# Two small VectorE operations written as operations of two tensors: the norms' clamp and the cast of a pair's tokens

## The chip, the cores and the metric

The kernel runs on one core of a Trainium2 chip. The metric is the device time of one execution in microseconds, the median of the runs shown. A core has TensorE (PE in the profile; its weight loads are PEld), VectorE (DVE), ScalarE (ACT), GpSimd (POOL) and SyncE (SP), which here only issues DMAs. Each engine works through its own list of instructions in order; semaphores tie the lists together.

## The reference

4096 tokens (16 sequences of 256) of width 128 pass through four stages, each preceded by a layer norm and added to its input: linear attention, a feed-forward part, column attention, and the same feed-forward part again. The feed-forward part is the one that matters here. It has two layers, and each layer is a local attention and an MLP:

```python
h = shift_token(x)
q, k, v = jnp.split(h @ wqkv, 3, axis=-1)          # 8 heads of 64
q = q / jnp.clip(jnp.linalg.norm(q, axis=-1, keepdims=True), 1e-12) * qs
...                                                # k likewise, with ksc
q, k = rotary_xpos(q, k)
o = local_attention(q, k, v)                       # windows of 64, softmax
x = x + o @ wo
...                                                # then shift, norm, w1, gelu gate, w2
```

The clamp of a norm is the `clip`: the kernel takes the larger of the sum of squares and 1e-24.

## The kernel before, in words

The program is a row of blocks: front and linear attention, then for each feed-forward part two attention blocks (`attention_block`) and two MLP blocks (`mlp_block`), and the column attention between the two parts. So there are four attention blocks and four MLP blocks. In every block each engine has a list of its own, written out by hand, and `wait_ge` and `then_inc` set the waits. There is no planner: the order in the code is the order on the engine.

Tokens are handled in 8 pairs of sequences (512 tokens each) and 32 tiles of 128 tokens. The attention loop runs over `i`; in its turn `i` an engine works on scores, softmax and output of unit `i` (or `i - 1`) and on the projections, rotary products and norms of tile `j = i + 5`. The parts that the change and the prediction's steps touch:

- **The cast** (`high_parts`, L458, DVE). A pair's shifted tokens `hs` (128x512, float32, in `K.rn[:, 1]`, put there by a DMA) are cast to float32r as `hhi`. POOL then takes the remainder `hlo` (`low_parts`, L516), and PE multiplies both parts with the weights (L384 to L386). It runs once a pair. In each attention block six casts are in the loop, at the end of DVE's turn for `i` = 0, 4, ... 20. The first two pairs' casts come earlier: for the first layer of a part in the entry of its attention block, between the layer norm's products (L714), and for the second layer within the MLP block before it (`early`), after x = 6 and x = 12.
- **The clamp** (`norms`, L439, DVE). L435 sums the squares of a tile's q and k per head into `ss16` (128x16, SBUF), L439 clamps them into `ssc`. It runs once a tile, 128 times in all. ACT takes the logarithm (L786) and the exponential (L790) of it, giving the factors `rnt`, and goes on with the squares of the next tile (L468). In the MLP blocks POOL raises `ssc` to the power -0.5 instead (L915); that is ten of the 128.
- **DVE's turn** in the loop: L426 (sine product of q), L700 twice (maxima), L706 (copy of transposed probabilities), L416 twice and L426 (the other rotary products), L435, L439 (the clamp), L710 (inverse sums), L449 (copy of keys), once a pair L719 (residual), and once a pair L458 (the cast).
- **POOL's turn**: L842 twice (probabilities times inverse sums, 128x512 each, released by L710), L507 twice (rotary sums times the norms' factors), once a pair L516, L498 twice (rotary sums of the tile ahead). All of these read and write SBUF.
- **ACT's turn**: L468 twice (squares), L478 (copy of values), L776 (copy of the other half of the transposed probabilities), eight exponentials (L768), L782, L488, L786, L790.
- **PE** transposes the probabilities (L621) as soon as each half of L842 is done, and among others does L406 (transposes), L611 (scores), L640 and L658.

Other lines that are spoken of: L277, a subtraction of two SBUF tensors into float32r on DVE in the norm before the column attention; L1081, L1083 and L1093 on DVE, L319, L327 and L329 (tables and weight parts for the next attention) on POOL in the MLP and entry stages; L568, the centring product of PE in the entry, which waits for L714 to free its bank.

Of the kernel before, what the change touches and what calls it, by code (L numbers as in the profile page):

```python
# [18 lines left out]
ALU = mybir.AluOpType  # L19
AX = mybir.AxisListType  # L20

P = 128
# [5 lines left out]
HEADS, DH, WINDOW = 8, 64, 64  # L28
# [8 lines left out]
NORM_MIN = 1e-24  # L37
# [41 lines left out]
def front_block(nc, K, A):  # L79

    S = K.s
# [6 lines left out]
    with nc.Block() as block:  # L88
        @block.sync
        def _(sp):  # L90
            x = d["L0_attn_a_x"].rearrange("b (u p) c -> p (b u) c", p=P)
            sp.dma_start(K.ident[:], d["c_ident"]).then_inc(S.ident_in, 16)
            for j in range(2):
                sp.dma_start(K.tok[:, 4 * j:4 * j + 4, :], x[:, 4 * j:4 * j + 4, :]).then_inc(S.x_in[j], 16)
            sp.dma_start(K.cent_w[:], d["c_cent"]).then_inc(S.cent_in, 16)
            sp.dma_start(K.mean_w[:], d["c_mean"]).then_inc(S.mean_in, 16)
            for j in range(2, PAIRS):
                sp.dma_start(K.tok[:, 4 * j:4 * j + 4, :], x[:, 4 * j:4 * j + 4, :]).then_inc(S.x_in[j], 16)
            sp.dma_start(masks[:, 0:2 * P], d["c_mask"]).then_inc(S.mask_in, 16)
            for r in range(2):  # L100
                sp.dma_start(masks[64 * r:64 * r + 64, 2 * P:4 * P], d["c_mask"][64 - 64 * r:128 - 64 * r]).then_inc(S.mask_in, 16)
            load_linear_weights(sp, K, A)

        @block.gpsimd
        def _(pool):
            pool.memset(K.eps[:], EPS_LN).then_inc(S.eps_set, 1)
            pool.memset(K.ssb[:], SS_BIAS)
            pool.memset(K.mhalf[:], -0.5)
            pool.memset(K.rsb[:], float(20.0 * np.log(2.0)))
            clear_linear_tiles(pool, K, A)  # L110
            for p in range(PAIRS):
                pool.wait_ge(S.ln_hi, p + 1)
                pool.tensor_tensor(K.LO[:, pair(p)], K.lnf[:, p % 2], K.HI[:, pair(p)].bitcast(F32), ALU.subtract).then_inc(S.ln_lo, 1)
# [317 lines left out]
def norms(dve, K, n, j):  # L431

    S = K.s
    dve.wait_ge(S.f_sq, 2 * TILES * n + 2 * j + 2)
    dve.tensor_reduce(K.ss16[:], K.sq.rearrange("p w (h d) -> p (w h) d", d=DH), AX.X, ALU.add).then_inc(S.f_ss, 1)  # L435
    dve.wait_ge(S.f_ss, TILES * n + j + 1)
    if j >= 1:
        dve.wait_ge(S.f_rn, TILES * n + j)
    dve.tensor_scalar(K.ssc[:], K.ss16[:], NORM_MIN, None, ALU.max).then_inc(S.f_cl, 1)  # L439


def keep_keys(dve, K, n, j, bank):
# [9 lines left out]
def high_parts(dve, K, n, q):  # L452

    S = K.s
    dve.wait_ge((S.f_h0, S.f_h1)[q % 2], 16 * PAIRS * n + 32 * (q // 2 + 1))
    if q >= 2:
        dve.wait_ge(S.f_v, TILES * n + 4 * (q - 1))
    dve.tensor_copy(K.hhi[:, q % 2], K.hs[:, q % 2]).then_inc(S.f_hi, 1)  # L458


def squares(act, K, n, j, banks):
# [409 lines left out]
def mlp_block(nc, K, n):  # L871
# [11 lines left out]
    with nc.Block() as block:  # L883
# [186 lines left out]
        def _(dve):  # L1070
# [32 lines left out]
            def early(x):  # L1103
                s, r = divmod(x - 8, 3)
                if x == 8:
                    dve.wait_ge(S.wa_tab, n + 2)
                if x in (6, 12):
                    high_parts(dve, K, n + 1, (x - 6) // 6)
                if 0 <= s < LEAD:
                    if r == 0:  # L1110
                        times_sin(dve, K, n + 1, s, 0, K.pt)
                        times_cos(dve, K, n + 1, s, 0, K.pt).then_inc(S.f_m, 1)
                    if r == 1:
                        times_cos(dve, K, n + 1, s, 1, K.pt)
                        times_sin(dve, K, n + 1, s, 1, K.pt).then_inc(S.f_m, 1)
                    if r == 2:
                        norms(dve, K, n + 1, s)
                if (x - 7) % 3 == 1 and 2 <= (x - 7) // 3 < LEAD + 1:
                    keep_keys(dve, K, n + 1, (x - 7) // 3 - 2, K.ss)
# [25 lines left out]
def clear_linear_tiles(pool, K, A):  # L1145

    pool.memset(A.bd[:], 0.0).then_inc(K.s.a_zero, 1)
    pool.memset(A.k2[:], 0.0)
    pool.memset(A.v[:], 1.0)
    pool.memset(A.eps[:], A_EPS)  # L1150
# [760 lines left out]
def linear_attention(nc, K):  # L1911
    with split_parts(nc, K, "linear"), ExitStack() as ctx:
        def sb(name, shape, dt=F32):
            return ctx.enter_context(nc.sbuf_tensor("linear_" + name, shape, dt))

        A = Bag()
        A.w = sb("w", [P, 4, P])
        A.b = sb("b", [P, 3])
        A.eps = sb("eps", [P, 1])
        A.bv = sb("bv", [P, P])  # L1920
        A.hm = sb("hm", [P, 16])
        A.bd = sb("bd", [P, 4 * A_F])
        A.w_hi = sb("w_hi", [P, 3, P], F32R)
        A.w_lo = sb("w_lo", [P, 3, P], F32R)
        A.q = sb("q", [P, 2, PAIR])
        A.k = sb("k", [P, 2, PAIR])
        A.v = sb("v", [P, 2, 4, A_M, 32])
        A.kp = sb("kp", [P, 4, A_HEADS * A_F])
        A.qp = sb("qp", [P, 2, A_M, PAIR])
        A.kvs = sb("kvs", [P, PAIR])  # L1930
        A.k2 = sb("k2", [P, 2, 2, A_M, 32])
        A.lnd = sb("lnd", [P, PAIR])
        A.rd = sb("rd", [P, PAIR])
        A.on = sb("on", [P, PAIR])
        front_block(nc, K, A)
        linear_attention_block(nc, K, A)


def column_attention(nc, K):
    with split_parts(nc, K, "column"), ExitStack() as ctx:  # L1940
        def sb(name, shape, dt=F32):
            return ctx.enter_context(nc.sbuf_tensor("column_" + name, shape, dt))

        B = Bag()
        B.w = sb("w", [P, 4, P])
        B.b = sb("b", [P, 4])
        B.bs = sb("bs", [P, 2])
        B.w_hi = sb("w_hi", [P, 3, P], F32R)
        B.w_lo = sb("w_lo", [P, 3, P], F32R)
        B.full = sb("full", [P, 2, PAIR])  # L1950
        B.hi = sb("hi", [P, 2, PAIR], F32R)
        B.lo = sb("lo", [P, 2, PAIR], F32R)
        B.qs = sb("qs", [P, 2, B_G, B_RUN], F32R)
        B.ks = sb("ks", [P, 2, B_G, B_RUN], F32R)
        B.kh = sb("kh", [P, 2, B_RUN // B_T, SEQ], F32R)
        B.E = sb("E", [P, 8, 2, SEQ])
        B.nm = sb("nm", [P, 8, 2])
        B.dn = sb("dn", [P, 8, 2])
        B.rd = sb("rd", [P, 4, 4, 2, 4])
        B.r = sb("r", [P, SEQ])  # L1960
        B.z = sb("z", [P, 2, SEQ])
        B.sel = sb("sel", [P, 2, P])
        B.dm = sb("dm", [P, B_T])
        B.o = sb("o", [P, SEQ])
        B.scr = nc.dram_tensor("qk_parts", [SEQS, B_ROWS, 4, B_DH, B_G, B_RUN], F32, kind="Internal").ap()
        norm_block(nc, K, 2, split=True, column=B)
        column_attention_block(nc, K, B)


def build(nc, d, out):  # L1970
    with ExitStack() as ctx:
        K = Bag()
        K.d, K.out = d, out
        K.s = Semaphores(lambda name: ctx.enter_context(nc.semaphore(name)))

        def sb(name, shape, dt=F32):
            return ctx.enter_context(nc.sbuf_tensor(name, shape, dt))

        def ps(name):
            return ctx.enter_context(nc.psum_tensor(name, [P, 512], F32))  # L1980

        K.X = sb("X", [P, TOK])
        K.Y = sb("Y", [P, TOK])
        K.tok = K.Y[:].rearrange("p (j c) -> p j c", c=P)
        K.ident = sb("ident", [P, P])
        K.identb = sb("identb", [P, P], BF16)
        K.mask = sb("mask", [P, 2, 2 * P], BF16)
        K.mean_w = sb("mean_w", [P, P])
        K.cent_w = sb("cent_w", [P, P])
        K.eps = sb("eps", [P, 1])  # L1990
        K.ssb = sb("ssb", [P, 1])
        K.mhalf = sb("mhalf", [P, 1])
        K.rsb = sb("rsb", [P, 1])
        K.colp = sb("colp", [P, 3])
        K.rn = sb("rn", [P, 2, 2, PAIR])
        K.pa = sb("pa", [P, 2, 2, PAIR])
        K.pb = sb("pb", [P, 2, 2, PAIR])
        K.rsum = sb("rsum", [P, 2, 2, PAIR])
        K.lnq, K.lnl, K.lnr, K.lnf = K.pb[:, 0], K.pb[:, 1], K.rsum[:, 0], K.rsum[:, 1]
        K.proj = [ps("proj0"), ps("proj1")]  # L2000
        K.sc = [ps("sc0"), ps("sc1")]
        K.pt = [ps("pt0"), ps("pt1")]
        K.ss, K.ob = ps("ss"), ps("ob")

        linear_attention(nc, K)
        ffn(nc, K, 0)
        column_attention(nc, K)
        ffn(nc, K, 1)
# [15 lines left out]
```

## Time and profile before

| | us |
|---|---|
| median of 3 runs | 1874.98 (1874.9 to 1876.33) |
| the profiled execution, whole | 1867.61 |
| its span, first to last instruction | 1865.8 |
| busy: PE / DVE / ACT / POOL | 1701.5 / 1376.7 / 1315.6 / 1117.5 |

The profile is of one execution. Its rows give start and duration of instructions, the idle time of the engine before each, and what ended that idle time. Consecutive instructions of an engine overlap by some tens of nanoseconds in the records, and PE's ends are modelled. The time of a POOL instruction is recorded more roughly than the others'. A duration counts from the start that is recorded to the end, so if an instruction is held up within the engine, its duration grows and no idle time is shown.

### The profile page before, as it was taken

What the parts mean: (1) busy time and instruction counts of PE and PEld (TensorE: products, weight loads), DVE (VectorE), ACT (ScalarE), POOL (GpSimd) and SP (SyncE); (2) the same over time, 40 slices, a digit from 0 to 9 for tenths busy, and PEclk for the clock granted to TensorE, in tenths of its full rate; (3) what the DMA queues carried; (4) which work ended last, traced back from release to release, by engine and by line L of the source; (5) the groups of instructions that cost most, each with busy time, mean ns of one, the idle gap of its engine ahead of it and who ended that gap; (6) DMA issues with size and microseconds to landing.
All of it is one profiled execution on the core that took longest, in us unless ns stands there. A gap on an engine that the chain in (4) does not pass through costs nothing. (4 is left out here: it accounts for less than half of the span.)

```text
span 1865.8 us, 43572 instructions
## 1 busy us (share of the span) xinstructions
PE 1701.5 (91%) x15560; PEld 1101.6 (59%) x15560; DVE 1376.7 (74%) x2369; ACT 1315.6 (71%) x4484; POOL 1117.5 (60%) x1002
## 2 busy tenths in 40 slices
PE   7998899998989999898599999799998899999989
PEld 4664677774657777454244444467776456777645
DVE  4554999983789999355488887699995488999645
ACT  4444788887358888644499998588887537888753
POOL 3554899982479999401222220699996178999620
PEclk7999999999999999999799999999999999999999
DMA  2002111103011110200765652211101202110201
GB/s 63 2 2 60 24 30 25 24 19 82 12 35 31 29 24 19 52 1 16 113 104 92 108 93 30 65 30 34 26 19 47 54 1 53 24 30 19 53 12 45
DMA packets 73214, 74.81 MB, mean 40 GB/s; under 512 B 18772, under 2 KB 56872, under 8 KB 70952
## 3 DMA queue, kind: packets, MB, share of 16 engines
q1 hardware_dynamic: 73000, 72.03, 18.8%
q8 instruction: 125, 2.05, 0.5%
q14 instruction: 89, 0.73, 0.1%
HBM read 27.99 MB, written 10.49 MB: 21 GB/s over the span
## 5 line engine op out<-in xcount | busy, mean ns | idle before, releaser
L498 POOL TENSOR_TENSOR rsum<-pa,pb 128x512 f32<-128x512 f32 x256 | 325.3, 1292 | 54.2 <-DVE pa L416 41.3
L768 ACT ACTIVATE ffn_prob<-sc,ffn_nmax 128x128 f32<-128x128 f32 x928 | 326.7, 387 | 5.3 <-DVE ffn_nmax L700 5.3
L842 POOL TENSOR_TENSOR ffn_prob<-ffn_prob,ffn_rden 128x512 f32<-128x512 f32 x256 | 265.2, 1057 | 75.2 <-DVE ffn_rden L710 75.0
L507 POOL TENSOR_TENSOR rsum<-rsum,ffn_rnt 128x512 f32<-128x512 f32 x256 | 261.4, 1042 | 10.9 <-ACT ffn_rnt L790 8.6
L768 ACT ACTIVATION_READ_ACCUMULATOR ffn_prob<-sc,ffn_nmax 128x1 f32 x928 | 210.5, 227 | 0.0
L426 DVE TENSOR_TENSOR pb<-proj,ffn_tab 128x512 f32<-128x512 f32 x236 | 161.1, 683 | 59.0 <-ACT rn L468 58.2
L406 PE MATMUL pt<-ident,rsum 128*128 128x128 f32 x960 | 154.6, 284 | 15.2 <-POOL rsum L507 12.5
L700 DVE TENSOR_REDUCE ffn_nmax<-sc 128x4 f32<-128x512 f32 x232 | 148.4, 680 | 13.6 <-PE sc L611 10.4
L406 PEld LDWEIGHTS pt<-ident,rsum 128*128 128x128 f32 x960 | 101.0, 141 | 96.7 <-ACT ffn_ptb L776 70.5
L621 PE MATMUL pt<-ident,ffn_prob 128*128 128x128 f32 x1024 | 144.5, 278 | 14.4 <-POOL ffn_prob L842 14.1
L1718 ACT ACTIVATE column_E<-proj,column_nm 128x256 f32<-128x256 f32 x256 | 123.4, 510 | 44.1 <-DVE column_nm L1642 43.7
L435 DVE TENSOR_REDUCE ffn_ss<-rn 128x16 f32<-128x1024 f32 x128 | 154.3, 1205 | 0.0
L640 PE MATMUL ob<-ffn_ptb,ffn_v 128*64 128x64 f32 (+1 forms) x3072 | 144.7, 244 | 9.1 <-issue 9.1
L640 PEld LDWEIGHTS ob<-ffn_ptb,ffn_v 128*64 128x64 f32 x3072 | 127.1, 138 | 42.5 <-issue 38.8
L416 DVE TENSOR_TENSOR pa<-proj,ffn_tab 128x512 f32<-128x512 f32 x236 | 150.5, 678 | 0.0
L621 PEld LDWEIGHTS pt<-ident,ffn_prob 128*128 128x128 f32 x1024 | 113.9, 141 | 46.6 <-POOL ffn_prob L842 35.9
L1040 ACT ACTIVATE ffn_prob<-proj,ffn_colb 128x512 f32<-128x512 f32 (+1 forms) x96 | 65.6, 687 | 101.7 <-PE proj L952 100.6
L658 PE MATMUL ss<-ffn_ot,ffn_wo 128*128 128x512 f32 x256 | 132.4, 599 | 2.7 <-ACT ffn_ot L782 2.7
L1093 DVE SCALAR_TENSOR_TENSOR ffn_ptb<-sc,ffn_colb,ffn_prob 128x512 f32<-128x512 f32 (+1 forms) x96 | 71.7, 747 | 79.7 <-ACT ffn_prob L1040 75.1
L776 ACT COPY ffn_ptb<-pt 128x512 f32<-128x512 f32 x128 | 75.1, 587 | 74.3 <-PE pt L621 74.3
L468 ACT ACTIVATE rn<-proj 128x512 f32<-128x512 f32 x236 | 125.8, 583 | 0.1
L1718 ACT ACTIVATE column_E<-sc,column_nm 128x256 f32<-128x256 f32 x256 | 124.5, 521 | 0.0
(272 smaller groups left out, 4368.2 us busy)
## 6 DMA issues: line engine op xcount, KB each, us to landing
ffn_v<-ffn_v SPq DMA_DIRECT2D x128, 128.0 KB, 2.3
column_ks<-qk_parts SPq DMA_DIRECT2D x64, 128.0 KB
rn<-Y SPq DMA_DIRECT2D x32, 128.0 KB, 2.3
qk_parts<-column_hi SPq DMA_DIRECT2D x64, 64.0 KB, 2.0
qk_parts<-column_lo SPq DMA_DIRECT2D x64, 64.0 KB, 2.0
column_qs<-qk_parts SPq DMA_DIRECT2D x32, 128.0 KB
column_qs<-qk_parts SPq DMA_DIRECT2D x64, 64.0 KB
rn<-Y SPq DMA_DIRECT2D x32, 127.5 KB, 2.4
```

The lines of the kernel that those rows point to most:

```text
L406: mm = pe.transpose(bank[:, tokens(c)], K.sm[:, j % 2, w, tokens(c)], K.ident[:])
L416: return dve.tensor_tensor(heads(K.m1[:, r, w]), heads(banks[w][:]), K.tab[:, t % 2, 2 * w].unsqueeze(1).broadcast_to([P, HEADS, DH]), ALU ...
L426: return dve.tensor_tensor(halves(K.m2[:, r, w]), halves(banks[w][:])[:, :, ::-1], K.tab[:, t % 2, 2 * w + 1].rearrange("p (a d) -> p a d" ...
L435: dve.tensor_reduce(K.ss16[:], K.sq.rearrange("p w (h d) -> p (w h) d", d=DH), AX.X, ALU.add).then_inc(S.f_ss, 1)
L498: pool.tensor_tensor(K.sm[:, r, w], K.m1[:, r, w], K.m2[:, r, w], ALU.add).then_inc(S.f_sum, 1)
L507: pool.tensor_tensor(heads(K.sm[:, r, w]), heads(K.sm[:, r, w]), K.rnt[:, r, w * HEADS:(w + 1) * HEADS].unsqueeze(2).broadcast_to([P, HEAD ...
L621: mm = pe.transpose(pt[e][:, tokens(k)], K.prob[:, i % 2, e, k], K.ident[:])
L640: mm = pe.matmul(K.ob[e * DH:(e + 1) * DH, s * SEQ + q0:s * SEQ + q1], K.v[:, b, 3 * s + k, hc], K.ptb[:, r, e, blk, q], start=True, stop= ...
L700: dve.tensor_reduce(K.nmax[:, i % 2, e], blocks(score_banks(i)[e][:]), AX.X, ALU.max, negate=True).then_inc(S.f_mx, 1)
L768: ins = act.activation(K.prob[:, r, e, k], score_banks(i)[e][:, tokens(k)], ACT.Exp, bias=K.nmax[:, r, e, k:k + 1], accum_out=K.den[:, r, ...
L842: pool.tensor_tensor(K.prob[:, r, e], K.prob[:, r, e], K.rden[:, r, e].unsqueeze(2).broadcast_to([P, 4, P]), ALU.mult).then_inc(S.f_pn, 1)
L1718: act.activation(B.E[:, slot, bt], score_banks[c][:, bt * SEQ:(bt + 1) * SEQ], ACT.Exp, bias=B.nm[:, slot, bt:bt + 1], accum_out=B.dn[:, s ...
```

## The change

DVE's clamp was an operation of one tensor and a constant; it becomes the larger of two tensors, the second a tile `floor` of 128x16 that POOL fills once with the constant at the program's start. The cast was a copy into another type; it becomes the larger of the tokens and themselves, written in the same type as before. Semaphores, waits and the places in DVE's order stay.

```diff
@@ front_block, POOL
             pool.memset(K.mhalf[:], -0.5)
+            pool.memset(K.floor[:], NORM_MIN)
@@ norms
-    dve.tensor_scalar(K.ssc[:], K.ss16[:], NORM_MIN, None, ALU.max).then_inc(S.f_cl, 1)
+    dve.tensor_tensor(K.ssc[:], K.ss16[:], K.floor[:], ALU.max).then_inc(S.f_cl, 1)
@@ high_parts
-    dve.tensor_copy(K.hhi[:, q % 2], K.hs[:, q % 2]).then_inc(S.f_hi, 1)
+    dve.tensor_tensor(K.hhi[:, q % 2], K.hs[:, q % 2], K.hs[:, q % 2], ALU.max).then_inc(S.f_hi, 1)
@@ build
         K.mhalf = sb("mhalf", [P, 1])
+        K.floor = sb("floor", [P, 2 * HEADS])
```

## Rows read from the trace of the kernel before

**Rows 1.** The page: span, and busy time of each engine
```profile
span 1865.8 us, 43572 instructions
...
PE 1701.5 (91%) x15560; PEld 1101.6 (59%) x15560; DVE 1376.7 (74%) x2369; ACT 1315.6 (71%) x4484; POOL 1117.5 (60%) x1002
```

**Rows 2.** Groups by line: busy us, mean ns | idle us before
```profile
L439 DVE TENSOR_SCALAR ffn_ssc<-ffn_ss 128x16 f32<-128x16 f32 x128 | 61.6, 481 | 4.4
...
L458 DVE CAST ffn_hhi<-rn 128x512 fp32r<-128x512 f32 x32 | 25.8, 805 | 4.9 <-DMA rn<-Y 4.9
...
L1093 DVE SCALAR_TENSOR_TENSOR ffn_ptb<-sc,ffn_colb,ffn_prob 128x512 f32<-128x512 f32 (+1 forms) x96 | 71.7, 747 | 79.7 <-ACT ffn_prob L1040 75.1 <-PE proj L952 3.3 <-PE sc L952 1.3
```

**Rows 3.** Single lines: duration ns min/median/max, first and last start us
```profile
L439 DVE TENSOR_SCALAR ffn_ssc<-ffn_ss x128: 174/290/1320, 187.7 to 1745.8; 128x16 f32<-128x16 f32 x128
...
L458 DVE CAST ffn_hhi<-rn x32: 416/922/925, 179.0 to 1702.4; 128x512 fp32r<-128x512 f32 x32
...
L277 DVE TENSOR_TENSOR column_LO<-rsum,column_HI x8: 691/693/693, 862.9 to 876.5; 128x512 fp32r<-128x512 f32 x8
...
L1083 DVE SCALAR_TENSOR_TENSOR ffn_glo<-ffn_qT,colp,ffn_ghi x32: 750/751/1671, 456.2 to 1850.7; 128x512 fp32r<-128x512 f32 x32
...
L327 POOL CAST ffn_wqkv_hi<-ffn_v x4: 611/946/1082, 182.2 to 1489.1; 128x512 fp32r<-128x512 f32 x4
```

**Rows 4.** Windows: stretch, length, busy us of each engine, PEclk, DMA
```profile
core 0: us, PE busy (x) PEld busy (x) DVE busy (x) ACT busy (x) POOL busy (x), PEclk, DMA share, GB/s
...
276.50:306.40 29.90, 29.55 (x362) 21.90 (x356) 27.86 (x47) 25.55 (x97) 27.66 (x26) 1.00 0.12 28
```

**Rows 5.** Timeline, DVE: start us, us, line, operation [idle before <-releaser]
```profile
276.58 0.92 DVE L458 CAST ffn_hhi<-rn 128x512 fp32r<-128x512 f32 x1
...
282.85 1.32 DVE L439 TENSOR_SCALAR ffn_ssc<-ffn_ss 128x16 f32<-128x16 f32 x1
...
290.87 0.29 DVE L439 TENSOR_SCALAR ffn_ssc<-ffn_ss 128x16 f32<-128x16 f32 x1
...
292.62 0.69 DVE L426 TENSOR_TENSOR pb<-proj,ffn_tab 128x512 f32<-128x512 f32 x1 [0.80 <-ACT rn L468]
...
306.49 0.92 DVE L458 CAST ffn_hhi<-rn 128x512 fp32r<-128x512 f32 x1
...
496.22 0.17 DVE L439 TENSOR_SCALAR ffn_ssc<-ffn_ss 128x16 f32<-128x16 f32 x1
```

**Rows 6.** Timeline, POOL, in the same pair
```profile
276.18 1.04 POOL L842 TENSOR_TENSOR ffn_prob<-ffn_prob,ffn_rden 128x512 f32<-128x512 f32 x1 [0.22 <-DVE ffn_rden L710]
...
277.18 1.22 POOL L842 TENSOR_TENSOR ffn_prob<-ffn_prob,ffn_rden 128x512 f32<-128x512 f32 x1
...
281.61 1.28 POOL L498 TENSOR_TENSOR rsum<-pa,pb 128x512 f32<-128x512 f32 x1
...
282.85 1.28 POOL L498 TENSOR_TENSOR rsum<-pa,pb 128x512 f32<-128x512 f32 x1
...
284.35 1.04 POOL L842 TENSOR_TENSOR ffn_prob<-ffn_prob,ffn_rden 128x512 f32<-128x512 f32 x1 [0.22 <-DVE ffn_rden L710]
...
289.83 1.29 POOL L498 TENSOR_TENSOR rsum<-pa,pb 128x512 f32<-128x512 f32 x1
```

**Rows 7.** Timeline, ACT, in the same pair
```profile
284.20 0.31 ACT L786 ACTIVATE ffn_lss<-ffn_ssc,ssb 128x16 f32<-128x16 f32 x1 [0.63 <-DVE ffn_ssc L439]
...
287.13 0.59 ACT L776 COPY ffn_ptb<-pt 128x512 f32<-128x512 f32 x1 [0.84 <-PE pt L621]
```

**Rows 8.** Timeline, DVE and POOL, around L1083 in an MLP stage
```profile
484.70 1.66 DVE L1083 SCALAR_TENSOR_TENSOR ffn_glo<-ffn_qT,colp,ffn_ghi 128x512 fp32r<-128x512 f32 x1
...
484.34 1.47 POOL L319 TENSOR_TENSOR ffn_tab<-ffn_v,ffn_cols 128x512 f32<-128x512 f32 x1
...
485.75 1.08 POOL L327 CAST ffn_wqkv_hi<-ffn_v 128x512 fp32r<-128x512 f32 x1
```

**Rows 9.** Timeline, PE: an entry stage, and an MLP stage
```profile
180.09 1.13 PE L568 MATMUL sc<-X,cent_w 128*128 128x512 f32 x2 [1.71 <-DVE Y L714]
...
484.53 0.47 PE L384 MATMUL pt<-ffn_wqkv_hi,ffn_hhi 128*128 128x512 f32 x1 [0.38 <-POOL ffn_hlo L516]
```

## The prediction

> **What bounds the kernel now.** I read the groups of instructions by line first. VectorE (DVE) is busy 1376.7 us of the 1865.8 us span, and the two operations that change are a small part of it: 61.6 us for the 128 clamps (L439) and 25.8 us for the 32 casts (L458) [rows 1, 2]. The reader should see that their means, 481 and 805 ns, say little: the clamp takes 174 ns at least, 290 at the median and 1320 at most, the cast 416, 922 and 925 [rows 3]. The same work takes up to seven times as long, so something outside the instruction decides.
>
> Then the windows, with the timeline of DVE beside them: inside an attention loop the cast comes once in four token tiles (a pair), at 276.58 and again at 306.49, so a pair takes 29.91 us [rows 5]. In such a stretch DVE is busy 27.86 and GpSimd (POOL) 27.66 us [rows 4]. Neither has much room, and TensorE's granted clock is full there, so the clock is no part of this.
>
> Then the timeline of one such pair, engine by engine. POOL's second L842 (277.18) takes 1.22 us where the one before it took 1.04, and the cast stands across their border: it starts at 276.58, the first L842 ends at 277.22, the cast at 277.50 [rows 5, 6]. So the cast waited for the first L842, needed 0.28 us more, and the second L842 waited for the cast. Cast and POOL operation exclude each other. The clamp at 282.85 met the tail of one sum (L498, ends 282.89), lost to the next sum, which starts level with it, and ended 0.04 us behind that one (284.13): 1.32 us for 16 elements. In the other three tiles it waits only for the rest of the second sum: 0.29 us at 290.87, where that sum ends at 291.12 [rows 5, 6]. A clamp with POOL quiet takes 0.17 us (496.22) [rows 5].
>
> Two chains close the loop. (a) DVE runs without a gap from the cast to the long clamp; clamp, logarithm and exponential (L786, L790) and square (L468) on ScalarE (ACT) release L426 of the next tile. (b) POOL runs without a gap from L842 at 276.18 through the sums to 284.13, then L842 at 284.35; its second half releases PE's transposes, those the copy L776, idle 0.84 us before it, then come eight exponentials, L786 and L468, and L426 at 292.62, for which DVE sat idle 0.80 us [rows 5 to 7]. Both start at the border of the two L842, where the cast is. That is why 0.3 us of cast counts.
>
> **The cast, 32 times.** Removed: 416 ns alone, 922 beside POOL. Added: an operation of two SBUF tensors of 512 elements into fp32r. The trace has it: L277, 691 to 693 ns, POOL quiet [rows 3]. Alone the edit costs 0.692 - 0.422 = 0.27 us. Does it also wait for POOL? The nearest row is L1083, which reads two SBUF tensors: 751 ns at the median, 1671 at most [rows 3]. At 484.70 it took 1.66 us. L319 on POOL ends at 485.81, L1083 at 486.36, and the next POOL operation, L327, takes 1.08 us where its least is 0.61 [rows 3, 8]. So two SBUF inputs wait and make POOL wait as the cast does; behind the release it needed 0.55 us, 0.20 less than its whole 0.75. The cast needed 0.28, 0.14 less than its 0.42. The new operation should need 0.69 - 0.14 = 0.55, so 0.64 + 0.55 = 1.19 us instead of 0.92: again +0.27. L327 after L1083 says that POOL's second L842 then ends 0.27 us later too. Bounds: if nothing of the 0.69 were hidden in the wait, +0.41; if it did not wait, 0.92 - 0.69 = -0.23.
>
> The Trainium skill speaks both ways here. The page Advanced Engine Details and Errata (VectorE Performance Modes) has only the two-port modes and GpSimd block each other; by it an operation of two tensors would go free, which is the second rival below. The page SBUF - State Buffer (Who interferes with whom) adds instructions with two SBUF inputs against GpSimd operations that read SBUF; with that the row of L1083 agrees, and the sum would be as taken.
>
> Where it lies: 24 of the 32 are in the four attention loops, six in each. Both chains start with it, DVE has no gap behind it and POOL none for 6.6 us, so both move by 0.27 and no slack absorbs it: 24 x 0.27 = 6.5 us. The idle times of 0.80 and 0.84 us are no cover, since what ends them moves as well. Four casts open the two entry stages: behind the first of each, PE's L568 sat idle 1.71 us for DVE's L714, which stands in DVE's order behind the cast, so 0.27; behind the second DVE waits for ACT anyway, but POOL's work starts from it, so between 0 and 0.27. I take 0.8 us for the four. Four lie in the MLP stages: PE's L384 sat idle 0.38 us for POOL's L516, which waits for the cast, so 0.27 for the first of each; half of that for the second, which has no such row [rows 9]. 0.8 us again.
>
> **The clamp, 128 times.** Alone it is 174 ns now. The new one has 16 elements in the same kind of operation as L277; no row has so few, and L1083 and L277 give no reason for a gain or a loss beyond some 10 ns. Bounds: -0.01 to +0.01 each, 1.3 us over 128; I take nothing. Its waits stay, since L1083 shows that two SBUF inputs wait for POOL too. Whether the long ones stay long hangs on who gets in first at 282.85. Both sides are timed from the end of the cast, by way of back-to-back work, and move by the same 0.27, so I expect them to meet as before, and the clamp to lose.
>
> The fill of `floor` is one more memset of 16 columns on POOL at the very start, before the inputs have arrived: nothing. No queue, DMA or semaphore changes.
>
> **Sum.** 6.5 + 0.8 + 0.8 = 8.1 us, or 0.43%, on the profiled execution's 1867.6 us (span 1865.8 and 1.8 around it): 1875.7. That execution is 7.4 us below the median of the runs shown, 1874.98, so against the median I say 1883.
>
> **The rivals.**
> 1. *The clamp gets in.* It needs no more than a few ns: it would start level with the second L498 and take 0.17 us instead of 1.32. For it: the meeting is level, and the new instruction may ask earlier. Against it: the long clamp recurs in every pair shown alike. The gain is mostly given back. The next L426 could come 0.63 us sooner (ACT's idle time before L786), but the one after it hangs on L842 at 284.35, which could start only when L498 ends, 0.21 us sooner [rows 6, 7]. 24 x 0.21 = 5 us, leaving 1878; if all of 0.63 counted, 15 us, leaving 1868. The rule of the page SBUF - State Buffer that whichever starts first gets the ports would let a clamp win as soon as it starts a few ns ahead; the level starts here show no winner by start alone.
> 2. *No waiting at all* (the other side of my forecast). The two-tensor form ignores POOL, and L1083's waits have another cause, such as its third, per-partition input. Then the cast takes 0.69 instead of 0.92 and the second L842 goes back from 1.22 to 1.04, which brings POOL's closed row 0.18 us forward; L842 at 284.35 loses its 0.22 us wait; the three other clamps give 0.12 each, of which I count half. 0.58 a pair, 24 times: 14 us, less the 1 us that the casts outside the loops cost. About 1862. It decides wherever a cast beside an L842 takes 0.69 us. Against it: L1093 has a per-partition input too, with one of its tensors in PSUM, and a mean of 747 ns over 96 [rows 2], so the per-partition input doesn't make the wait.
> 3. *The cast's cost is absorbed* by some slack behind it. Then only the stages outside the loops pay: 1875 to 1877. Against it: no gap in rows 5 and 6 that isn't itself timed from the cast.
> 4. *The cast loses its race too*, to the second L842: up to 1.0 us more for each of 24 (it would end 0.55 us behind 278.22), about 1907. Against it: L1083 won the same race against L327.
>
> **How the numbers follow.** Forecast 0.70; rival 1: 0.13; rival 2: 0.08; rival 3: 0.05; rival 4: 0.04. About 0.2%, 3.7 us, is what a measurement of this kernel can tell from no change. The forecast and rival 4 are slower, less a little for a forecast that comes out under 3.7 us: 0.72. Same: most of rival 1, rival 3 and that little, 0.15. Faster: rival 2 and the far end of rival 1, 0.13. The range: upward 24 x 0.41 plus 1.6 and 1.3 for the clamps gives 12.7, so 1888. Downward to the middle of rival 1 (0.42 x 24 = 10 us off the forecast): 1873. Rivals 2 and 4 and the end of rival 1 stay outside.
>
> **What would show it.** L458 as an operation of two tensors: 0.69 us at the least, 1.19 at the median; L842 with a maximum near 1.49; L439 unchanged at 0.17, 0.29 and 1.32, still one long in four; the windows of a pair 30.17 us instead of 29.90. A cast of 0.69 beside L842 refutes the waiting. A clamp maximum near 0.5 is rival 1. A pair that stays at 29.90 with casts of 1.19 is rival 3.

## The result, and the profile after

| | before | changed |
|---|---|---|
| median of 20 runs, us | 1873.6 (1867.35 to 1878.22) | 1880.17 (1875.67 to 1884.62) |
| ratio, 95% interval | | 1.0037 (1.0027 to 1.0047) |
| profiled execution, whole, us | 1867.61 | 1884.62 |
| its span, us | 1865.8 | 1882.8 |

The changed kernel is slower by 0.37%, which is 6.9 us (5.1 to 8.8); the two medians as they stand are 6.6 us apart. The two profiled executions differ by 17.0 us, more than the medians do, so they can't be subtracted as a whole: before's, at 1867.61 us, is as fast as all but one of the 20 runs, the changed kernel's is the slowest of its own. They have to be read stretch by stretch.

From the page of the changed kernel, the lines that answer to [rows 1]:

```profile
span 1882.8 us, 43573 instructions
...
PE 1708.9 (91%) x15560; PEld 1102.6 (59%) x15560; DVE 1385.2 (74%) x2369; ACT 1318.1 (70%) x4484; POOL 1125.3 (60%) x1003
```

DVE is busy 8.5 us more and POOL 7.8 us more. All lines of the changed kernel stand one lower than before: the clamp is L440, the cast L459, the second factor of the probabilities L843.

Its single lines, with durations in ns as min/median/max, which answer to [rows 3]:

```profile
L440 DVE TENSOR_TENSOR ffn_ssc<-ffn_ss,floor x128: 174/291/1319, 191.2 to 1761.1; 128x16 f32<-128x16 f32 x128
...
L459 DVE TENSOR_TENSOR ffn_hhi<-rn x32: 681/1185/1190, 181.2 to 1717.3; 128x512 fp32r<-128x512 f32 x32
...
L843 POOL TENSOR_TENSOR ffn_prob<-ffn_prob,ffn_rden x256: 1039/1042/1490, 221.0 to 1790.5; 128x512 f32<-128x512 f32 x128
```

and the same of L842 in the kernel before:

```profile
L842 POOL TENSOR_TENSOR ffn_prob<-ffn_prob,ffn_rden x256: 1035/1040/1224, 216.4 to 1775.2; 128x512 f32<-128x512 f32 x128
```

The cast went from 416/922/925 to 681/1185/1190. L843, the POOL operation next to it, has a median within 2 ns of the old one and a maximum 266 ns higher. The clamp stands where it stood, 174/290/1320 before and 174/291/1319 now.

The window of one pair (stretch, length, busy us of PE, PEld, DVE, ACT and POOL, granted clock, share of DMA), against [rows 4]:

```profile
281.50:311.70 30.20, 29.86 (x352) 21.88 (x352) 28.17 (x47) 25.60 (x97) 27.95 (x26) 1.00 0.12 28
```

DVE's timeline in the same pair, against [rows 5]:

```profile
281.81 1.19 DVE L459 TENSOR_TENSOR ffn_hhi<-rn 128x512 fp32r<-128x512 f32 x1
...
288.35 1.32 DVE L440 TENSOR_TENSOR ffn_ssc<-ffn_ss,floor 128x16 f32<-128x16 f32 x1
...
296.38 0.29 DVE L440 TENSOR_TENSOR ffn_ssc<-ffn_ss,floor 128x16 f32<-128x16 f32 x1
...
298.14 0.69 DVE L427 TENSOR_TENSOR pb<-proj,ffn_tab 128x512 f32<-128x512 f32 x1 [0.81 <-ACT rn L469]
...
312.02 1.19 DVE L459 TENSOR_TENSOR ffn_hhi<-rn 128x512 fp32r<-128x512 f32 x1
```

and POOL's, against [rows 6]:

```profile
281.41 1.04 POOL L843 TENSOR_TENSOR ffn_prob<-ffn_prob,ffn_rden 128x512 f32<-128x512 f32 x1 [0.22 <-DVE ffn_rden L711]
...
282.41 1.49 POOL L843 TENSOR_TENSOR ffn_prob<-ffn_prob,ffn_rden 128x512 f32<-128x512 f32 x1
...
287.11 1.29 POOL L499 TENSOR_TENSOR rsum<-pa,pb 128x512 f32<-128x512 f32 x1
...
288.37 1.27 POOL L499 TENSOR_TENSOR rsum<-pa,pb 128x512 f32<-128x512 f32 x1
...
289.86 1.04 POOL L843 TENSOR_TENSOR ffn_prob<-ffn_prob,ffn_rden 128x512 f32<-128x512 f32 x1 [0.22 <-DVE ffn_rden L711]
```

The cast starts at 281.81. The first L843 ends at 282.45, the cast at 283.00, 0.55 us behind. The second L843 is recorded at 282.41, but takes 1.49 us instead of 1.22 and ends at 283.90. From there POOL runs closed to 289.64, and the long clamp ends with the second sum, at 289.67. The next cast starts at 312.02, 30.21 us after the first; it was 29.91.

Two of the eight casts outside the loops, one in an entry stage and one in an MLP stage:

```profile
181.23 0.69 DVE L459 TENSOR_TENSOR ffn_hhi<-rn 128x512 fp32r<-128x512 f32 x1 [4.60 <-DMA rn<-Y]
...
491.56 0.68 DVE L459 TENSOR_TENSOR ffn_hhi<-rn 128x512 fp32r<-128x512 f32 x1
```

Both are 0.26 us longer than before (0.43 at 179.01, 0.42 at 482.62). But DVE sat idle 4.60 us for the DMA in front of the first, where it was 2.67 in the kernel before. That stands ahead of anything the first cast can change, and it moves the rest of the execution by 2 us.

One more thing differs from stretch to stretch outside the pairs, in both kernels: TensorE's granted clock. Here are two stretches of 4 us of the kernel before, with the columns of the window above, each from 58.5 us behind the sixth cast of an attention loop, in the first loop and in the third:

```profile
424.80:428.80 4.00, 4.00 (x70) 3.00 (x70) 1.14 (x2) 3.66 (x18) 1.68 (x2) 1.00 0.89 209
...
1426.70:1430.70 4.00, 4.00 (x63) 3.36 (x63) 0.00 (x0) 3.04 (x17) 1.64 (x2) 0.57 0.89 207
```

In the third loop the clock is at its lower level, 1.2 GHz, for 3.4 us of this stretch (0.57 is the mean of the 4 us); in the first it stays at 2.4 GHz. DVE's next L706 waits 4.86 us for PE's transposes there where it waits 3.30 in the first loop:

```profile
427.66 0.69 DVE L706 COPY ffn_ptb<-pt 128x512 f32<-128x512 f32 x1 [3.30 <-PE pt L621]
...
1431.09 0.69 DVE L706 COPY ffn_ptb<-pt 128x512 f32<-128x512 f32 x1 [4.86 <-PE pt L621]
```

From the sixth cast to the end of the loop's last L842 it is 72.40 us without this fall and 73.85 to 73.88 with it. I call this stretch a loop's tail. The profiled execution of before has the fall in three of its four tails, that of the changed kernel in two. Why one tail has it and another has not, no run shows: TensorE had been busy for 1.74 of the 4 us up to 425 in the first loop, and for 1.74 of the 4 us up to 1427 in the third.

### The profile page after: what moved, and what is told of

The parts are those of the page before. It is cut to its first block and busy times, and to the rows that moved or that the text cites. A ratio compares the mean times of both kernels' runs of the same rounds, so it can differ in the third digit from the quotient of the medians.

```text
span 1882.8 us, 43573 instructions
## 1 busy us (share of the span) xinstructions
PE 1708.9 (91%) x15560; PEld 1102.6 (59%) x15560; DVE 1385.2 (74%) x2369; ACT 1318.1 (70%) x4484; POOL 1125.3 (60%) x1003
## 5 line engine op out<-in xcount | busy, mean ns | idle before, releaser
L843 POOL TENSOR_TENSOR ffn_prob<-ffn_prob,ffn_rden 128x512 f32<-128x512 f32 x256 | 271.9, 1083 | 74.8 <-DVE ffn_rden L711 74.5
L427 DVE TENSOR_TENSOR pb<-proj,ffn_tab 128x512 f32<-128x512 f32 x236 | 161.5, 684 | 58.4 <-ACT rn L469 58.0
L622 PE MATMUL pt<-ident,ffn_prob 128*128 128x128 f32 x1024 | 150.5, 281 | 16.5 <-POOL ffn_prob L843 16.2
```

Of the source, the lines that this page charges most:

```text
L427: return dve.tensor_tensor(halves(K.m2[:, r, w]), halves(banks[w][:])[:, :, ::-1], K.tab[:, t % 2, 2 * w + 1].rearrange("p (a d) -> p a d" ...
L622: mm = pe.transpose(pt[e][:, tokens(k)], K.prob[:, i % 2, e, k], K.ident[:])
L843: pool.tensor_tensor(K.prob[:, r, e], K.prob[:, r, e], K.rden[:, r, e].unsqueeze(2).broadcast_to([P, 4, P]), ALU.mult).then_inc(S.f_pn, 1)
```

## The experiments

The two casts at the ends of the first loop are five pairs apart. Their starts give the length of a pair in each kernel, free of what happens outside the loops. Over the four loops the lengths within one kernel differ by 0.06 to 0.18 us, with the first and the third the longest in nearly every kernel, so the first loop is compared with the first loop. "Long" counts the clamps of over 1 us. "Falls" counts the loops' tails, of four, in which TensorE's clock fell in the profiled execution; it is a count of one execution, while the ratio comes from medians.

| kernel | first and sixth cast, us | a pair, us | long | falls | ratio (95%) |
|---|---|---|---|---|---|
| before | 216.76, 366.32 | 29.91 | 24 | 3 | |
| changed | 221.40, 372.43 | 30.21 | 24 | 2 | 1.0037 (1.0027 to 1.0047) |
| e1_clamp_tt | 220.96, 370.61 | 29.93 | 23 | 0 | 1.000 (0.9988 to 1.0011) |
| e2_cast_tt | 220.30, 371.15 | 30.17 | 24 | 0 | 1.0048 (1.0031 to 1.0064) |
| e3_clamp_red | 218.13, 365.94 | 29.56 | 0 | 0 | 0.9918 (0.9898 to 0.9938) |
| e4_cast_red | 220.26, 368.89 | 29.73 | 21 | 4 | 0.9998 (0.9987 to 1.001) |
| e7_hybrid | 215.77, 362.68 | 29.38 | 0 | 4 | 0.9916 (0.9898 to 0.9933) |
| e8_order | 216.91, 363.88 | 29.39 | 21 | 2 | 0.9934 (0.9917 to 0.9952) |
| e9_hybrid_order | 215.58, 362.21 | 29.33 | 0 | 4 | 0.9913 (0.9892 to 0.9933) |
| e10_pool_later | 218.88, 368.83 | 29.99 | 1 | 0 | one run, 1872.38 us |
| e11_before_nudge | 218.82, 367.55 | 29.75 | 3 | 2 | 0.9994 (0.9978 to 1.0011) |
| e12_after_nudge | 217.03, 366.98 | 29.99 | 1 | 0 | 1.0013 (0.9998 to 1.0027) |

### The two parts by themselves: e1 and e2

e1 is the kernel before with the clamp's half of the change (and the fill of `floor`), e2 with the cast's half.

```diff
e1: -    dve.tensor_scalar(K.ssc[:], K.ss16[:], NORM_MIN, None, ALU.max).then_inc(S.f_cl, 1)
e1: +    dve.tensor_tensor(K.ssc[:], K.ss16[:], K.floor[:], ALU.max).then_inc(S.f_cl, 1)
e2: -    dve.tensor_copy(K.hhi[:, q % 2], K.hs[:, q % 2]).then_inc(S.f_hi, 1)
e2: +    dve.tensor_tensor(K.hhi[:, q % 2], K.hs[:, q % 2], K.hs[:, q % 2], ALU.max).then_inc(S.f_hi, 1)
```

> The clamp alone as an operation of two tensors, the cast as before. My theory: the clamp costs nothing, since alone both forms take 174 ns and both wait for POOL: L440 again 174/290/1320 ns with one long wait in four tiles, a pair of tiles 29.91 us, ratio to before 1.000 (within 0.001). Rival, that the clamp carries part of the loss (it asks for the port at another moment, or holds POOL up longer): a pair over 29.95 us and a ratio of 1.001 to 1.002. Rival, that it gets in ahead of the second sum: no clamp over 0.6 us, ratio 0.997.

> The cast alone as an operation of two tensors, the clamp as before. My theory: the whole change is here: the cast 0.69 us alone and 1.19 beside L842, a pair 30.20 us instead of 29.91, 24 x 0.29 = 7.0 us and some tenths outside the loops, ratio 1.0037 to 1.0045. Rival, that clamp and cast share the loss: ratio 1.002 or less. Rival, that the 10 us by which the two profiled executions differ outside the loops belong to the cast: ratio over 1.007.

e1's clamp:

```profile
L440 DVE TENSOR_TENSOR ffn_ssc<-ffn_ss,floor x128: 174/288/1322, 191.9 to 1745.4; 128x16 f32<-128x16 f32 x128
```

e2's cast:

```profile
L458 DVE TENSOR_TENSOR ffn_hhi<-rn x32: 681/1186/1189, 181.0 to 1712.9; 128x512 fp32r<-128x512 f32 x32
```

The clamp's form costs nothing that shows: the same durations, 23 long ones, a pair 0.02 us longer, ratio 1.000. Over all four loops its pairs are 0.08 us shorter to 0.06 longer than before's, 0.00 in the mean. The cast's form is the loss: a pair is 0.26 us longer and the ratio, 1.0048, has the changed kernel's 1.0037 within its interval. Both of e2's rivals fall: a shared loss wanted 1.002 or less, a loss mostly outside the loops over 1.007, and the interval holds neither.

### The clamp in a form that doesn't wait: e3

```diff
     pool.memset(K.mhalf[:], -0.5)
+    pool.memset(K.ss2[:], NORM_MIN)
...
-    dve.tensor_reduce(K.ss16[:], K.sq.rearrange("p w (h d) -> p (w h) d", d=DH), AX.X, ALU.add).then_inc(S.f_ss, 1)
+    dve.tensor_reduce(K.ss2[:, :, 0], K.sq.rearrange("p w (h d) -> p (w h) d", d=DH), AX.X, ALU.add).then_inc(S.f_ss, 1)
...
-    dve.tensor_scalar(K.ssc[:], K.ss16[:], NORM_MIN, None, ALU.max).then_inc(S.f_cl, 1)
+    dve.tensor_reduce(K.ssc[:], K.ss2[:], AX.X, ALU.max).then_inc(S.f_cl, 1)
```

> The cast as before; the clamp as a maximum over pairs of columns (a tensor_reduce with one SBUF input, L435 writing every second column of a tile whose other columns hold the constant), a form that shows no waiting for POOL in the trace of before (L435, 1.20 us whether POOL works or not). Theory that the waiting comes from the form's port and not from its place: every clamp about 0.20 us, none long. Then the gain: if chain (b) gives most of the long wait back, a pair is 0.2 us shorter for the long wait and some 0.1 to 0.2 for the short ones, 29.5 to 29.7 us, 24 x 0.2 to 0.4 = 5 to 10 us, ratio 0.995 to 0.9975. Rival, nothing given back: 0.63 and three times 0.1, 0.9 us a pair, 22 us, ratio 0.988. Rival, clamps still long: ratio 1.000.

Its clamp:

```profile
L440 DVE TENSOR_REDUCE ffn_ssc<-ss x128: 185/186/189, 189.2 to 1734.9; 128x16 f32<-128x32 f32 x128
```

DVE's timeline in the tile that had the long clamp, and the one behind it:

```profile
283.54 0.19 DVE L440 TENSOR_REDUCE ffn_ssc<-ss 128x16 f32<-128x32 f32 x1
...
285.46 0.69 DVE L427 TENSOR_TENSOR pb<-proj,ffn_tab 128x512 f32<-128x512 f32 x1 [0.47 <-ACT rn L469]
...
293.03 0.69 DVE L427 TENSOR_TENSOR pb<-proj,ffn_tab 128x512 f32<-128x512 f32 x1 [1.28 <-ACT rn L469]
```

and POOL's there:

```profile
283.51 1.29 POOL L499 TENSOR_TENSOR rsum<-pa,pb 128x512 f32<-128x512 f32 x1
...
284.76 1.05 POOL L843 TENSOR_TENSOR ffn_prob<-ffn_prob,ffn_rden 128x512 f32<-128x512 f32 x1
```

The clamp takes 0.19 us everywhere, beside POOL's sums too. So the waiting belongs to the instruction's form and not to its place. And most of the gain is given back, as the prediction's first rival had it: the clamp is 1.13 us shorter, but a pair only 0.35. L843 now starts as the sum ends (283.51 + 1.29 = 284.80; recorded 284.76) instead of 0.22 us behind it, and the rest of what DVE saved has become idle time in front of L427, 0.47 us in this tile where there was none and 1.28 in the next where there was 0.80 [rows 5]. 24 pairs of 0.35 us are 8 us; the ratio says 15 (12 to 19). Part of the difference stands in the tails of the profiled executions: e3's four are 72.1 us each, none with a fall of the clock, where three of before's are 73.9 with one, which makes 4 us. That much in each of the executions behind the medians is not shown; e1 has no fall in its profile either, and its ratio is 1.000. So the rest of the ratio stays open.

### The cast in a form that doesn't wait: e4 and e7

e4 casts with a reduction over an axis of length one. e7 is e3 with e4's cast for the last six of the eight pairs and the copy of before for the eight casts outside the loops.

```diff
-    dve.tensor_copy(K.hhi[:, q % 2], K.hs[:, q % 2]).then_inc(S.f_hi, 1)
+    dve.tensor_reduce(K.hhi[:, q % 2], K.hs[:, q % 2].unsqueeze(2), AX.X, ALU.max).then_inc(S.f_hi, 1)
```

> The clamp as before; the cast as a tensor_reduce over an axis of length one (one SBUF input, 512 elements). Theory that one input and no second port needs no waiting: the cast 0.69 us in every place, L842 back to 1.04 at most; POOL's closed row comes 0.18 us forward, a pair 29.73 us, 24 x 0.18 = 4.4 us, ratio 0.9975. If DVE's chain decides alone: 0.17 us a pair at most, the same size. Rival, that it waits for POOL like the other forms: 1.19 us and ratio 1.004, like the cast of two tensors.

> The clamp in the form of e3 (0.19 us everywhere) and the cast in the form of e4 for the pairs in the loops, a copy as before for the eight casts outside them, where POOL is mostly idle and the copy's 0.42 us is shorter than the 0.67. Theory that both port waits cost separately: the pair 29.4 us, 0.14 to 0.18 below e3's 29.55, so 24 x 0.5 = 12 us below before, ratio 0.990 to 0.9935. Rival, that with the clamp no longer waiting the cast's 0.18 us are hidden (POOL waits for DVE, not the other way round): the pair 29.55 us as in e3 and the ratio of e3.

e4's cast and its neighbour on POOL:

```profile
L458 DVE TENSOR_REDUCE ffn_hhi<-rn x32: 666/670/686, 180.4 to 1705.7; 128x512 fp32r<-128x512 f32 x32
...
L842 POOL TENSOR_TENSOR ffn_prob<-ffn_prob,ffn_rden x256: 1037/1041/1045, 219.9 to 1778.4; 128x512 f32<-128x512 f32 x128
```

With the same 512 elements and nearly the same time alone as the operation of two tensors (666 against 681 ns), this form never waits and never makes L842 wait: the maximum is 686 ns, and L842's is 1045. The pair is 0.18 us shorter, as worked out. So the slower rate is not what made the changed cast wait. What is left is the second tensor input or the operation itself, which no run separates; and having one input is not enough to go free, since the copy has one and waits. The ratio did not follow: 0.9998, with 0.9975 outside its interval. Of the eight casts outside the loops, the four with POOL quiet take 0.26 us more than the copy; the other four, where the copy itself waited, take from 0.15 more to 0.18 less. That is 1.0 us together, and brings the expectation to 0.998, still outside. In the profiled execution TensorE's clock fell in all four tails, which take 73.6 to 73.7 us: one fall of 1.5 us more than in before's execution. With it the expectation would be 0.999, within the interval; that the medians' executions have such falls as often is not shown.

e7's first and sixth cast:

```profile
215.77 0.68 DVE L460 TENSOR_REDUCE ffn_hhi<-rn 128x512 fp32r<-128x512 f32 x1
...
362.68 0.68 DVE L460 TENSOR_REDUCE ffn_hhi<-rn 128x512 fp32r<-128x512 f32 x1
```

146.91 us over five pairs, 29.38 each, 0.18 below e3: in the pairs the cast's gain comes on top of the clamp's. Its ratio, 0.9916, can't be told from e3's. The two profiled executions show where such a gain can go: the twenty pairs between the first and the sixth casts are 3.8 us shorter in e7, but its four tails take 73.3 to 73.4 us each, with a fall of the clock in every one, against 72.1 in e3. That is 5.1 us more, and the spans are 1854.4 and 1854.0 us.

### Which chain carries the clamp's wait: e8 and e9

e8 is the kernel before with the inverse sums in front of the clamp (`between` is `inverses(i)` in the loop); e9 is e7 with the same order.

```diff
 def norms(dve, K, n, j, between=None):
...
+    if between is not None:
+        between()
     dve.wait_ge(S.f_ss, TILES * n + j + 1)
```

> The kernel before with the inverse sums (L710) put in front of the clamp, both behind L435, forms as before. L710 no longer stands behind the clamp's wait: L842 starts 0.2 to 0.3 us earlier in three tiles of four, and in the fourth as soon as L498 ends (0.2 us). If chain (b) of the prediction (L842, transposes, L776, exponentials, L786) decides where the long wait's gain is given back, a pair is 0.3 to 0.7 us shorter, ratio 0.991 to 0.996, though the clamp itself still waits 0.1 and 1.1 us. Rival, that chain (a) decides, clamp to L786 to L468: a pair the same or 0.1 us longer, ratio 1.000 to 1.002.

> e7 and e8 together. If the two gains are the same one (L842 no longer kept by the clamp's wait): as e7, within 0.1 us a pair, ratio 0.990 to 0.993. If they add: another 0.1 us for each tile in which ACT waits for PE, a pair 29.0 to 29.2 us, ratio 0.985 to 0.989.

e8's DVE in the tile with the long clamp:

```profile
281.86 0.19 DVE L712 RECIPROCAL ffn_rden<-ffn_den 128x8 f32<-128x8 f32 x1
...
281.98 1.13 DVE L441 TENSOR_SCALAR ffn_ssc<-ffn_ss 128x16 f32<-128x16 f32 x1
...
291.37 0.69 DVE L426 TENSOR_TENSOR pb<-proj,ffn_tab 128x512 f32<-128x512 f32 x1 [0.67 <-ACT rn L470]
```

and its POOL:

```profile
281.80 1.28 POOL L500 TENSOR_TENSOR rsum<-pa,pb 128x512 f32<-128x512 f32 x1
...
283.04 1.03 POOL L844 TENSOR_TENSOR ffn_prob<-ffn_prob,ffn_rden 128x512 f32<-128x512 f32 x1
```

The clamp still waits 1.13 us here, and yet a pair is 0.52 us shorter and the ratio 0.9934. L844 starts at 283.04, as the sum ends (283.08), since L712 was done at 282.05. Chain (a) alone would have left the pair as it was or made it 0.1 us longer, so what the clamps' waits cost the kernel before is for the most part L710's place behind them, in the order DVE, L842, transposes, L776, exponentials: chain (b). The 0.52 us are not the long clamp's alone, though: the edit frees L710 in all four tiles, the long clamp itself takes 1.13 us instead of 1.32, and the cast, now beside an earlier L844, takes 0.73 us instead of 0.92 in 22 of the 24 cases. How they share the gain is not shown. e9 confirms the chain from the other side: with clamp and cast no longer waiting, the new order adds 0.06 us a pair. It is the same gain, not a second one.

### How narrow the clamp's race is: e10, e11, e12

One memset of a single column on POOL, once a pair, ahead of the two sums. e10 and e12 are the changed kernel with it, e11 the kernel before.

```diff
+                if i % 4 == 1 and i >= 1:
+                    pool.memset(K.nudge[:], 0.0)
                 if 0 <= j < TILES:
                     sums(pool, K, n, j)
```

> The changed kernel with one memset of a single column (about 0.09 us) put on POOL between L517 and the two sums L499 of the tile whose clamp waits long, so that the second sum starts about 0.1 us after the clamp instead of level with it. It measures how narrow the race is. If whichever asks first gets in: the clamp ends soon after the first sum, no clamp over 0.6 us in the loops, and L499 grows to 1.4 us or so once a pair; the pair 30.1 us (0.1 us of memset on POOL's closed row, 0.2 us back from the long wait). If POOL holds on between two operations that follow each other at once, or the clamp asks over 0.1 us after its recorded start: a clamp of 1.4 us and a pair of 30.3 us.

> The kernel before, both forms as they were, with the one-column memset of e10 on POOL. In e10 the clamp of two tensors got in when the second sum began 0.04 to 0.05 us after it. If the moment decides and not the form: the old clamp gets in as well, 0.18 us where it took 1.32, and a pair is 29.7 us (29.91 less the 0.21 that e10's pair is shorter than the changed kernel's), ratio 0.997 to 0.998. Rival, that the form of two tensors takes part of the port only and so gets in more easily: the old clamp stays at 1.4 us, a pair 30.0 us, ratio 1.001.

> The kernel of e10 again, now timed. Its pair of 29.97 to 29.99 us against 29.91 before says 24 x 0.07 = 2 us slower than before in the loops, and some tenths outside: ratio 1.001 to 1.002, against 1.0037 for the changed kernel without the memset.

POOL of e10 in a pair:

```profile
284.12 0.09 POOL L863 MEMSET nudge<- 128x1 f32 x1
...
284.18 1.29 POOL L499 TENSOR_TENSOR rsum<-pa,pb 128x512 f32<-128x512 f32 x1
...
285.43 1.28 POOL L499 TENSOR_TENSOR rsum<-pa,pb 128x512 f32<-128x512 f32 x1
...
286.67 1.04 POOL L843 TENSOR_TENSOR ffn_prob<-ffn_prob,ffn_rden 128x512 f32<-128x512 f32 x1
```

and the clamps of that tile and the next on DVE:

```profile
285.38 0.18 DVE L440 TENSOR_TENSOR ffn_ssc<-ffn_ss,floor 128x16 f32<-128x16 f32 x1
...
292.62 0.61 DVE L440 TENSOR_TENSOR ffn_ssc<-ffn_ss,floor 128x16 f32<-128x16 f32 x1
```

The second sum is recorded 0.05 us after the clamp, and the clamp got in: 0.18 us. In the changed kernel the sum came 0.02 us after it, and the clamp took 1.32. e11 shows the same of the old form, clamp first and sum behind it:

```profile
225.08 0.17 DVE L439 TENSOR_SCALAR ffn_ssc<-ffn_ss 128x16 f32<-128x16 f32 x1
...
225.12 1.28 POOL L498 TENSOR_TENSOR rsum<-pa,pb 128x512 f32<-128x512 f32 x1
```

Over all such meetings in these traces (a sum that starts within 0.1 us of a clamp), the changed kernel's 24 clamps lost with the sum from 21 ns ahead of them to 17 ns behind; with the memset, 66 of 68 got in with the sum 25 to 56 ns behind (23 in e10, 21 in e11, 22 in e12; e11 lost at 38 and at 52), and the two that met the sum closer, at 10 ns in e10 and at 0 in e12, lost. So in the main the moment decides and not the form, and some 0.02 us lie between losing and winning. One thing came out otherwise than expected: a sum that starts behind a clamp that got in was to grow to 1.4 us, and it stays at 1.28. The pair of e10 is 0.22 us shorter than the changed kernel's, memset included: the first rival's mechanism, and close to its price, 0.21. Part of the long wait comes back as a wait of 0.61 us in the next tile, since POOL and DVE then meet elsewhere. e12's ratio, 1.0013, came out as expected from the pair; e11's pair is 29.75, and of the 0.997 to 0.998 that I expected its ratio's interval holds only the upper end.

In the trace, then, the side that is recorded some 0.05 us ahead gets in and a lead of 0.02 us is not enough. The Trainium skill's page SBUF - State Buffer (Who interferes with whom) lets whoever issues first take the ports for the whole instruction. In e10 and e11 the side that is ahead gets in, as it says, but the sum behind the clamp's 0.18 us shows no wait. And 20 of the changed kernel's 24 clamps are recorded ahead of the sum and lost, so by the recorded starts alone the rule does not hold there; whether the two engines ask in another order than the records have, no run shows.

## Why the prediction was right, and by how much

- **The wait of two SBUF inputs** was inferred from L1083 alone. It holds: the cast's median is 1185 ns where I worked out 1.19 us, the least 681 where I had 0.69, and it ends 0.55 us behind L843, as taken. e4 adds what the prediction didn't have: a tensor_reduce, with one SBUF input, runs as slowly and doesn't wait.
- **POOL's share**: L843 at 1.49 us at most, as worked out from L327.
- **No slack behind the cast**: a pair 30.17 us was forecast; 30.21 measured, 30.17 with the cast alone. 24 times 0.29 is 7.0 us where I had 6.5, and e1 leaves 0.02 us a pair for the clamp in the first loop, 0.00 over all four. The loops alone make up the 6.9 us of the ratio. How close that comes is partly luck: the same sum misses e3's ratio by 7 us and e4's by 4, and a fall of TensorE's clock moves a tail by 1.5 us.
- **The clamp** costs nothing (e1), and its long waits stayed: 24 of them before and after.
- **Outside the loops** I had 1.6 us. One row bears it out: from the third to the fourth cast outside the loops the trace of before has 18.58 us (482.62 to 501.20), that of the changed kernel 18.86 (491.56 to 510.42), 0.28 for one cast. In the first entry the second cast starts 1.54 us behind the first before and 1.81 behind it now. As a whole the term can't be checked. The medians leave 0 us for it with an interval of 2 us to each side, and the profiled executions differ there by more than any cast could give: by 2.2 us before the first cast already. The 8.1 us that were forecast lie within the interval of the 6.9 found (5.1 to 8.8), so the difference needs no reason of its own.
- **The clock.** The prediction left TensorE's clock out because it is full in the pairs. That holds for the pairs; outside them it falls in some tails and not in others, at 1.5 us a tail, and the sum has no term for it.
- **Rival 1** had the right price (0.21 us a pair, 0.22 in e10) and its condition was nearly met: the latest sum that still won started 17 ns behind its clamp, the earliest that lost with the memset 25 ns behind. I said that both sides are timed from the end of the cast and would meet as before. They did, to within some 20 ns; the argument held, but that a shift of this size stayed on the losing side is luck, since no row of before had the margin.
- **Rival 2** fell with the first L459 beside L843 that took 1.19 us; **rival 3** with the pair; **rival 4** with the cast's maximum of 1190 ns.

## What to carry to other kernels

Look at the spread of an instruction's duration before its mean: a form that takes 174 ns in one place and 1320 in another is waiting inside the engine, where no idle time shows it. On DVE beside a busy POOL, an operation of two SBUF tensors is no way out: it waited and made POOL wait as the copy did, and ran longer. A tensor_reduce with one input did not wait in any place tried, and for the clamp that paid (0.9918); for the cast it made the pairs shorter and left the whole as it was (0.9998). Moving what others wait for (here L710) ahead of the instruction that waits paid as well (0.9934). And a gain in the loop that was looked at can be lost in another stretch: here TensorE's clock, full in every pair, fell in some of the tails.

## What the runs showed that I had not expected

A one-column memset of 0.09 us, added to an engine with no gap in that stretch, made the changed kernel's pair 0.22 us shorter (30.21 to 29.99). And in e10 the clamp was not held up by the first sum at all, though that sum is recorded until 285.47 and the clamp started at 285.38 and took 0.18 us: POOL's recorded end lies behind the moment from which DVE can go ahead. In the kernel before, 0.14 us of the cast's 0.42 were hidden in the wait in the same way.

The fastest kernel here is e9, 0.9913 of before (0.9892 to 0.9933); e7 and e3 can't be told from it, and e8, at 0.9934, hardly.
